# Output steps two places earlier, quadratic scores first, a drain in another order and logits in eight matmuls

## The reference

```
x = LN(x + linear_attention(x))           # 8 heads, elu+1 features, relu MLP
x = LN(x + moe64(x))                      # 64 experts, top 8 of 64, capacity 64 tokens each, shared expert
x = LN(x + gated_attention(x))            # below
x = LN(x + moe8(x))                       # 8 experts, top 2 of 8, all experts for all tokens
```

```
v, gate = split(silu(norm(x) @ Wh + bh))             # 256 features each
quad_q, lin_q, quad_k, lin_k = four affine copies of silu(norm(x) @ Wqk + bqk)
attn = relu(quad_q @ quad_k.T / 32 + bias)**2        # inside a group, lower triangle
out  = attn @ v + lin_q @ (sum over earlier groups of lin_k.T @ v / 32)
x    = (gate * out) @ Wout + bout + x
```

```
p = softmax(x @ Wg.T); top 2, normalised to sum 1 -> comb[t, e]
for e in 8 experts: a, b = split(x @ W1[e].T + b1[e]);  out += comb[:, e] * ((a * sigmoid(b)) @ Wo.T + bo)
```

## Time and profile before

| | us |
|---|---|
| median of 3 runs (lowest, highest) | 703.17 (703.03, 703.64) |
| the profiled execution | 702.37 |
| its span | 700.6 |
| PE busy | 587.2 (84%) |
| DVE busy | 437.3 (62%) |
| POOL busy | 442.0 (63%) |
| ACT busy | 274.0 (39%) |
| mean granted TensorE clock | 0.852 |

### The profile page before, as it was taken

One profiled execution on the slowest core, in us unless ns is written; L12 is line 12 of the kernel. 1 busy time (PEld: TensorE's weight loads), 2 busy tenths in 40 slices (PEclk: granted clock), 3 DMA queues, 4 the chain that ended last, 5 costly groups with the idle time before them and its releaser, 6 DMA issues.

```text
span 700.6 us, 10473 instructions
## 1 busy us (share of the span) xinstructions
PE 587.2 (84%) x3201; PEld 473.7 (68%) x3201; DVE 437.3 (62%) x1480; ACT 274.0 (39%) x559; POOL 442.0 (63%) x479
## 2 busy tenths in 40 slices
PE   5998999379299986365999989988989899999882
PEld 4797888335188775255777777867877787788662
DVE  2465778689634435534576767667667666775762
ACT  3465565215122223331634435345435353363331
POOL 6353444617677775644777867967868859652573
PEclk9999899659755555587999989999989989999996
DMA  4697475579022124330300300300203000000000
GB/s 121 175 300 292 190 270 220 195 170 206 10 72 65 60 67 146 124 120 1 121 1 9 127 1 8 128 9 13 115 8 127 1 8 8 1 16 0 10 7 16
DMA packets 47221, 61.98 MB, mean 88 GB/s; under 512 B 13026, under 2 KB 39873, under 8 KB 46146
## 3 DMA queue, kind: packets, MB, share of 16 engines
q1 hardware_dynamic: 44610, 56.15, 25.3%
q0 software_dynamic: 2560, 5.23, 2.6%
HBM read 35.16 MB, written 24.13 MB: 85 GB/s over the span
## 4 chain that ended last, share of the span: by engine, by line
PE 57%; DVE 18%; issue 8%; ACT 8%; DMA 4%; POOL 3%; SPq 1%; DVEq 0%; POOLq 0%; ACTq 0%
PE pair L1218 8%; PE pair L1220 7%; PE pair L1219 7%; PE pair L1450 5%; DVE c_g L1071 3%; DVE cand L1649 3%; PE pair L1460 2%; DVE keyT L1651 2%; PE pair L1324 2%; PE pair L467 2%; PE pair L1313 2%; PE pair L1717 2%; PE pair L1318 2%; ACT c_sg L940 2%; PE pair L511 2%
## 5 line engine op out<-in xcount | busy, mean ns | idle before, releaser
L854 POOL TENSOR_TENSOR c_acc<-c_acc,c_g 128x512 f32<-128x512 f32 x112 | 144.0, 1286 | 65.9 <-DVE c_g L1071 60.4
L940 ACT ACTIVATE c_sg<-pair 128x512 f32<-128x512 f32 x128 | 76.4, 597 | 161.6 <-PE pair L1220 161.3
L1071 DVE SCALAR_TENSOR_TENSOR c_g<-pair,c_comb,c_sg 128x256 f32<-128x256 f32 x224 | 97.6, 478 | 63.9 <-ACT c_sg L940 62.7
L1218 PE MATMUL pair<-c_w_hi,c_x3h 128*128 128x512 f32 x256 | 117.0, 457 | 9.3 <-DVE c_g L1071 6.6
L1220 PE MATMUL pair<-c_w_hi,c_x3l 128*128 128x512 f32 x256 | 105.8, 413 | 0.0
L1219 PE MATMUL pair<-c_w_lo,c_x3h 128*128 128x512 f32 x256 | 105.6, 412 | 0.0
L1218 PEld LDWEIGHTS pair<-c_w_hi,c_x3h 128*128 128x128 f32 x256 | 52.0, 203 | 25.6 <-DVE c_g L1071 13.4
L1220 PEld LDWEIGHTS pair<-c_w_hi,c_x3l 128*128 128x128 f32 x256 | 51.1, 200 | 12.7
L1219 PEld LDWEIGHTS pair<-c_w_lo,c_x3h 128*128 128x128 f32 x256 | 52.1, 204 | 8.0
L1534 POOL DMA_INDIRECT rows_all<-token_rows,tok_row x32 | 31.2, 976 | 12.6 <-issue 8.2
L1539 POOL DMA_INDIRECT routed_rows<-x1T_all,dest_row x32 | 32.3, 1008 | 9.8 <-issue 8.5
(11 more groups left out here) (326 smaller groups left out, 1499.0 us busy)
## 6 DMA issues: line engine op xcount, KB each, us to landing
routed_rows<-rows_all SPq DMA_DIRECT2D x8, 2048.0 KB
c_c<-routed_rows SPq DMA_DIRECT2D x7, 2048.0 KB, 7.7
token_rows<-a_xw SPq DMA_DIRECT2D x8, 384.0 KB, 3.1
a_x<-in_L_attn_x SPq DMA_DIRECT2D x8, 256.0 KB, 3.3
base_all<-a_xw SPq DMA_DIRECT2D x8, 256.0 KB, 3.5
c_c<-routed_rows SPq DMA_DIRECT2D x4, 512.0 KB, 5.1
out<-c_outb SPq DMA_DIRECT2D x16, 128.0 KB, 1.8
wgu_late<-in_L_ffn_w_gate SPq DMA_DIRECT2D x4, 480.0 KB, 7.1
```

The source lines that it names most:

```text
L854: g.tensor_tensor(acc, acc, b["g"][:, (2 * uf + i) % 4, :, :], ALU.add).then_inc(s["acc"], 1)
L940: a_.activation(b[f"sg{q % 2}"][:, :, :], self.pair[q % 2][:, :, H1:2 * H1], SIG).then_inc(s["sig"], 1)
L1071: ins = v.scalar_tensor_tensor(out=dst, in0=self.pair[q % 2][:, x, 0:H1], scalar=b[f"comb{uf}"][:, j * E1 + e:j * E1 + e + 1], in1=b[f"sg{ ...
L1218: t.matmul(dst, w_hi, x_hi, start=start, stop=False)
```

## The change

Seven things are done.

- **Output of half 0.** Its transposes go from place 10 to 8 and stand behind the value product there; its product with Wo and its half sums go from place 11 to 9, the product ahead of the w product. What belongs to half 1 stays.
- **Scores.** The four quadratic 128x128 matmuls come first, with a count of their own, and wait only for the products that they read; the linear ones follow. ACT does relu and square before it copies off1, which has its own semaphore now. `atd` goes from place 7 to 6.
- **Norm scale.** POOL computes the norm factors of half 1 of batch t behind the 128x1024 addition of the contributions instead of ahead of it.
- **Logits.** The high and low parts of Wg stand beside each other in one tile (`wg_hl`), so that the high part of x3 meets both in one matmul of 16 columns and the low part meets the high one in another of 8: eight matmuls, not twelve. DVE adds the two halves in a `tensor_reduce`, and the gating has 12 steps.
- **Drain.** For k >= 8, DVE does the aggregation ahead of the maxima and the norm additions ahead of the keys; in the last batch the shifted logits come behind the mask.
- **W1 on POOL.** `setup_pool_w1` waits for the last keys (`keys_written`).
- **Names.** Two blocks of PE's code become functions.

```diff
-AT = dict(zT=0, accT=(10, 1), out=(11, 2), gate=2, y4=(11, 3), quads=3, gate2=3, v=4, outb=(15, 5), sim=6, off=7, atd=7, av=8, w=9, x3=10, x3T=12, lg=13, y=7, z=11)
-
-GATING = {13: (1, 2, 3, 4), 14: (5, 6, 7, 8), 15: (9, 10, 11)}
-GATE_STEPS = 11
+AT = dict(zT=0, accT=(8, 1), out=(9, 2), gate=2, y4=(9, 3), quads=3, gate2=3, v=4, outb=(15, 5), sim=6, off=7, atd=6, av=8, w=9, x3=10, x3T=12, lg=13, y=7, z=11)
+
+GATING = {13: (1, 2, 3, 4, 5), 14: (6, 7, 8, 9), 15: (10, 11, 12)}
...
                     ins = v.match_replace(zap[:, j, :], b["top"][:, j, :], lg[:, j, :], NEG)
                 ins.then_inc(s["pick"], 1)
+
+            if k < self.N:
+                if 0 <= m < self.N:
+                    pick_top()
+                if 0 <= n < self.N:
+                    aggregate()
+            else:
+                if 0 <= n < self.N:
+                    aggregate()
+                if 0 <= m < self.N:
+                    pick_top()
+            if 0 <= m < self.N:
+                dve.wait_ge(s["pick"], 5 * m + 1)
+                if m < self.N - 1:
+                    from_top()
+                strike()
             n = k
             if n < self.N:
                 dve.wait_ge(s["kv_mm"], n + 1)
@@ -402,6 +423,8 @@
                 if m > 1:
                     dve.wait_ge(s["maskT_mm"], m // 2)
                 v.tensor_tensor(b["mask"][:, :, m % 2, :], zap, lg, ALU.not_equal).then_inc(s["mask_sb"], 1)
+                if m == self.N - 1:
+                    from_top()
             n = k - 1
             if 0 <= n < self.N:
                 dve.wait_ge(s["sqm_sb"], n + 1)
...
+
+            if k < self.N and 0 <= m and m % 2:
+                write_keys()
+            if 0 <= n < self.N:
+                add_norms()
+            if k >= self.N and m < self.N and m % 2:
+                write_keys()
 
     def pe(self, pe):
         t, b, s, bank, pair, ident = self.nc.tensor, self.b, self.s, self.bank, self.pair, self.ident
...
@@ -720,6 +752,7 @@
     def setup_pool_w1(self, pool):
         g, k, chain = self.nc.gpsimd, self.k, self.pool_chain
         pool.wait_ge(self.w1_loaded, 16)
+        pool.wait_ge(self.keys_written, PAIRS)
         chain(g.tensor_copy(k["w127"][:, :], k["w1n"][:, :, D - 1]))
         for q in range(4):
...
@@ -870,11 +903,12 @@
                 g.tensor_tensor(c[:, :, 0:512], c[:, :, 0:512], c[:, :, 512:1024], ALU.add).then_inc(s["sum_step"], 1)
             if f is not None:
                 add_experts(f, uf, 0, 1)
+            if not summed:
+                pool.wait_ge(s["sum_step"], 3 * r - 2)
+                g.tensor_tensor(c[:, :, 0:256], c[:, :, 0:256], c[:, :, 256:512], ALU.add).then_inc(s["sum_step"], 1)
             if t is not None:
                 rstd_f(t, 1)
             if not summed:
-                pool.wait_ge(s["sum_step"], 3 * r - 2)
-                g.tensor_tensor(c[:, :, 0:256], c[:, :, 0:256], c[:, :, 256:512], ALU.add).then_inc(s["sum_step"], 1)
                 pool.wait_ge(s["sum_step"], 3 * r - 1)
                 pool.wait_ge(s["z"], r)
                 yv = b["y"][:, :].rearrange("p (j d) -> p j d", d=D)
@@ -973,12 +1007,12 @@
                         act.wait_ge(s["gate_mm"], 3 * a + 3)
                         gate(a, 2, X)
                     if q == AT["sim"]:
-                        act.wait_ge(s["off_mm"], 2 * a + 1)
-                        a_.copy(b["off1"][:, :], Z[:, :])
                         act.wait_ge(s["t1"], a + 1)
                         a_.activation(b["rl"][:, :, :], b["t"][:, :, :], ACT.Relu).then_inc(s["relu"], 1)
                         act.wait_ge(s["relu"], a + 1)
                         a_.activation(b["rl"][:, :, :], b["rl"][:, :, :], ACT.Square).then_inc(s["t2"], 1)
+                        act.wait_ge(s["off_mm"], 2 * a + 1)
+                        a_.copy(b["off1"][:, :], Z[:, :]).then_inc(s["off1"], 1)
                     if q == AT["off"]:
                         act.wait_ge(s["off_mm"], 2 * a + 2)
...
@@ -1110,37 +1144,40 @@
             if step == 1:
                 dve.wait_ge(s["lg_mm"], a + 1)
                 v.memset(self.landing(), 0.0)
-                for j in range(NT):
-                    ins = v.max(top[:, j, :], t3(lg)[:, j, :])
+                ins = v.tensor_reduce(t3(lg), Z[:, 256:256 + 2 * n].rearrange("p (j h e) -> p j e h", h=2, e=E1), AX.X, ALU.add)
             else:
...
@@ -1174,12 +1211,12 @@
                         prod(a, 2, X, b["gateT"][:, 1, :])
                     if q == AT["sim"]:
 
-                        dve.wait_ge(s["diag_mm"], a + 1)
+                        dve.wait_ge(s["diag_mm"], 2 * a + 1)
                         t_, ml = b["t"][:, :, :], Y[:, :].rearrange("p (j i) -> p j i", i=P)
                         v.tensor_tensor(t_, X[:, :].rearrange("p (j i) -> p j i", i=P), bcast_mid(k["biasT"][:, :], NT), ALU.add).then_inc(s["t1"], 1)
+                        dve.wait_ge(s["diag_mm"], 2 * a + 2)
                         v.tensor_tensor(ml, ml, bcast_mid(k["ltmask"][:, :], NT), ALU.mult).then_inc(s["ml"], 1)
                     if q == AT["atd"]:
-                        t_, ml = b["t"][:, :, :], Y[:, :].rearrange("p (j i) -> p j i", i=P)
                         dve.wait_ge(s["ml"], a + 1)
                         dve.wait_ge(s["t2"], a + 1)
                         v.tensor_tensor(t_, b["rl"][:, :, :], ml, ALU.add).then_inc(s["atd"], 1)
@@ -1241,6 +1278,25 @@
                 tok = slice(j * P, (j + 1) * P)
                 ins = split3(self.pair[q % 2][:, x, :], b[f"x3h{uf}"][:, tok], b[f"x3l{uf}"][:, tok], b["w1_hi"][:, e, :], b["w1_lo"][:, e, :])
             ins.then_inc(s["u_mm"], 1)
+
+        def half_transposes(n, un, half):
+            pe.wait_ge(s["acc"], 14 * n + 7 * (half + 1))
+            if half or not first(n):
+                pe.wait_ge(s["outb"], 2 * n + half)
+            for x in range(2):
+                for h in range(2):
+                    c = slice((2 * x + h) * P, (2 * x + h + 1) * P)
+                    ins = t.transpose(bank[4][:, c], b[f"acc{un}"][:, 2 * half + x, h * P:(h + 1) * P], ident[:, :])
+            ins.then_inc(s["accT_mm"], 1)
+
...
@@ -1294,10 +1338,14 @@
                         split3(X[:, :], hi[:, HID + P:2 * HID], lo[:, HID + P:2 * HID], zh[:, :], zl[:, :]).then_inc(s["gate_mm"], 1)
                     if q == AT["sim"]:
                         pe.wait_ge(s["quads"], a + 1)
+                        pe.wait_ge(s["prod5"], 5 * a + 3)
+                        for j in range(NT):
+                            tok = slice(j * P, (j + 1) * P)
+                            ins = t.matmul(X[:, tok], b["qk"][:, tok], b["qq"][:, tok], start=True, stop=True)
+                        ins.then_inc(s["diag_mm"], 1)
                         pe.wait_ge(s["prod5"], 5 * a + 5)
                         for j in range(NT):
                             tok = slice(j * P, (j + 1) * P)
-                            t.matmul(X[:, tok], b["qk"][:, tok], b["qq"][:, tok], start=True, stop=True)
                             ins = t.matmul(Y[:, tok], b["lk"][:, tok], b["lq"][:, tok], start=True, stop=True)
                         ins.then_inc(s["diag_mm"], 1)
                         t.matmul(Z[:, 0:384], b["lk"][:, 0:P], b["lq"][:, P:L], start=True, stop=True)
@@ -1307,6 +1355,7 @@
                         t.matmul(X[:, 0:256], b["lk"][:, P:2 * P], b["lq"][:, 2 * P:L], start=True, stop=True).then_inc(s["off_mm"], 1)
                     if q == AT["av"]:
                         pe.wait_ge(s["atd"], a + 1)
+                        pe.wait_ge(s["off1"], a + 1)
                         pe.wait_ge(s["off2"], a + 1)
                         for h, dst in ((0, Y), (1, Z)):
                             c = slice(h * P, (h + 1) * P)
...
                                 ins = t.matmul(dst[:, j * P:(j + 1) * P], b["v"][:, j, c], b["t"][:, j, :], start=False, stop=(j == NT - 1), skip_group_check=True)
                             ins.then_inc(s["av_mm"], 1)
+                if f is not None and q == AT["accT"][0]:
+                    half_transposes(f, uf, 0)
+                if a is not None:
                     if q == AT["w"]:
                         pe.wait_ge(s["go"], 2 * a + 2)
                         for j in range(NT):
@@ -1333,7 +1385,9 @@
                         xh, xl = b[f"x3h{ua}"], b[f"x3l{ua}"]
                         for j in range(NT):
                             tok = slice(j * P, (j + 1) * P)
-                            ins = split3(Z[:, j * E1:(j + 1) * E1], xh[:, tok], xl[:, tok], k["wg_hi"][:, :], k["wg_lo"][:, :])
+                            at = 256 + j * 2 * E1
+                            t.matmul(Z[:, at:at + 2 * E1], xh[:, tok], k["wg_hl"][:, :], start=True, stop=False, skip_group_check=True)
+                            ins = t.matmul(Z[:, at:at + E1], xl[:, tok], k["wg_hl"][:, 0:E1], start=False, stop=True, skip_group_check=True)
                         ins.then_inc(s["lg_mm"], 1)
 
```

(12 more changed lines are left out.)

78 lines of the change are left out of this document (37 added, 41 removed).

## The result

The changed kernel takes 681.88 us, median of 4 runs (681.09 to 683.88), against 703.1 for the kernel before in the same comparison; the ratio is 0.9725, 95% interval 0.9686 to 0.9764. The profiled execution took 681.64, its span is 679.9, 20.7 less than the span before.

A forecast was written before the change was run, and what follows sets the result against it. Bodies bound by PE's matmuls, idle time and low clock; the first half by DVE's search and POOL's gathers. +2.5 - 4.5 - 0.85 - 4.9 - 8.8 + 2.7 = -13.85 from 702.37: 688.5, median 689; range 681 to 698.

The forecast's parts named there:

- Front, +2.5: Up to the first gather: last keys 2.05 us earlier, but POOL's W1 work waits for them, gather 2.5 us later.
- low pieces: Stretches of 3.41 us at granted clock 0.50; nine counted in the bodies, two taken to be left.
- Rival 2: POOL makes up its delay before the slots are ready, first gather 2 us earlier: 684.5 us; chance 0.09.
- First attention, -4.5: First attention body, uncovered by experts: split scores start the value product 3.6 us earlier, and part of its 1.7 is won.
- its logits, -0.85: First body's logits: four fewer matmuls at half clock save 0.85 us.
- Places 8 to 13, -4.9: Seven bodies at -0.7 us each: the 0.75 hole before the value product goes, smaller holes come at places 12 and 13.
- The walk: One body stepped through with its rows' durations: half sums ahead of y3 delay x3; logits at 557.2 instead of 557.90.
- Logits to transposes, -8.8: First logit to half-1 transposes, seven bodies: -12.0 us if the clock never falls, +3.2 for two low pieces left.
- Rivals 1, 3 and 4: Clock falls as before (692, chance 0.25); at place 12 and logits (about 700, 0.12); stays low between them (about 712, 0.04).
- Tail, +2.7: Ninth body: half-0 transposes at place 8 wait 2.5 us for POOL's seventh sum; bounds +2.1 and +3.5 (clock falls).

The follow-up runs named there:

- e7: The kernel before, run again with a trace and no edit: one run, 696.1 us.
- e5: The changed kernel without POOL's wait for the last keys: 677.14 us, ratio 0.9634.
- e3: The changed kernel with the scores in the old order (quadratic and linear alternating, off1 ahead of relu, atd at place 7): 693.9 us, ratio 0.9885.
- e2: The changed kernel with each 16-column logits matmul cut into two of 8 columns, twelve again: 681.92 us, ratio 0.9702.
- e1: The changed kernel with the output of half 0 back at places 10 and 11: 680.94 us, ratio 0.9701.
- e0: The changed kernel again, no edit: 682.86 us, ratio 0.9724.
- e9: e8 with the half sums of half 0 at place 11 instead of 9: 704.2 us, ratio 0.9826.
- e11: e8 with the half sums of half 0 at place 10 instead of 9: 710.87 us, ratio 0.9909.
- e4: The changed kernel with half 0's transposes and output back at places 10 and 11 in the ninth body only: 678.9 us, ratio 0.9665.
- e10: The kernel before with only the new order of the scores: 705.02 us, ratio 0.9819.
- e8: The changed kernel with the edits of e4 and e5 together: 692.6 us on a chip where before takes 719.15, ratio 0.9651.

## Why the prediction came out as it did

**Front, +2.5.** Right in mechanism and sign. The drain gained 1.65 (2.05 said), the new wait moved the gather from the slots to POOL, +1.63 at like clock (e7 against after), and the first normed transposes +2.1. The first trace of before had two low pieces at 70 us, worth 2.3 at the keys and 1.2 at the gather, which is why the two profiled executions differ by 0.4 there. Rival 2, POOL making up its delay, did not happen, and e5 puts the price of the wait at 3.

**First attention, -4.5, and its logits, -0.85.** Measured -4.3 and -0.86; e3 and e2 show that they are the scores and the four matmuls. In the other traces with the new scores first attention is 4.7 to 5.9 shorter, so that -4.3 is the least of them.

**Places 8 to 13, -4.9.** Measured -5.7, holes of 1.00, 0.37 and 0.71 where 1.25, 0.5 and 0.35 were said. The scores are 6.7 of it (e3), and the earlier output costs 1.0 the other way (e1 against e0). The walk had the half sums ahead of y3 as a cost. They are one, small, and what they free is larger: e9 and e11 show that either of the two next places makes a hole of 1.7 to 2.7.

**Logits to transposes, -8.8.** The term that was mis-sized: -12.6. Two bodies of before in e7 that ran at 1.00 throughout take 8.20 and 8.18 from logits to transposes, and the same bodies now 8.02 and 8.03: so about 1 us of the 12.6 is other than the clock, and nine low pieces cost the rest, 1.3 each, an estimate from these. The mechanism, no long hole and so no fall of the clock, holds in eight traces of eight with the half sums at place 9; I had left two of nine low pieces, and put the gain on the output as a whole, where e9 puts it on DVE's half sums; in six traces of six with a hole of 1.7 or more in each body there are four to nine. The two pieces left over stood on no row, and they are most of what the term missed. How the chip decides this the runs don't tell; single holes of 1.9 pass without a fall. The inner working was off too. I took off 0.45 for four matmuls and put on 0.45 for four transposes, and neither counts, as DVE paces this stretch (e2: under 0.1 a body on average); the errors cancel. Rivals 1, 3 and 4 had the clock fall in the seven bodies, and it did not. Rival 2's 684.5 is the nearest number to the time measured, but its mechanism did not happen.

**Tail, +2.7.** The wait was 2.30 (2.5 said), the whole 4.2 against the first trace, 3.9 against e4: the clock is low for 3.41 us right behind the wait, from 650.35 on, and the bound that I gave for that, +3.5, was 0.4 to 0.7 too low. The traces of e2 and e3 have the same wait of 2.3 and no low piece behind it, and take 32.17 us from the eighth body's transposes to the last ones, where after takes 33.51 and e4 29.62: so the wait costs 2.55, as said, and the clock 1.34.

**Not in the sum.** DVE's halt of 2.5 us at a loop turn, which was in the trace of before and which I did not ask about: -2.5. From the forecast's -13.85: logits to transposes -3.8, the halt -2.5, places 8 to 13 -0.8, the front -1.8, first attention +0.2, the second body's start +0.4, the tail +1.5 make -20.65, and the span shows -20.7.

**The noise.** The prediction had runs tell a change from none at 0.2%, from three runs within 0.6 us. The fourth was 697.78, and the interval of the comparison is 0.4% to either side.

## What to carry to other kernels

Look for the one long wait of TensorE in a repeated stage and for what its neighbour engine does just ahead of releasing it; work of that engine that nobody waits for soon belongs in front of the wait's chain, even where the walk shows new small holes. A move that is good where another stage covers it (output at place 8) can cost in the one iteration without cover; give that iteration its own place. And take a second trace of the kernel before ahead of a sum: of the 7 us that the forecast was off, 2.5 were a halt that comes in every trace of that kernel and 1.4 a low clock early on that came in one of two, and one trace can't tell which is which.

## What the hardware showed that I had not expected

The clock stayed at 1.00 for 321 us on end (329.5 to 650.3), with holes of up to 1.06 us in it; two traces of the same kernel differed by two low pieces in the first stage (6.8 us, 1.4 of them left at the first normed transposes). A DVE halt of 2.4 to 2.6 us, without a wait in the profile, comes at one turn of the loop over the bodies in both traces of before and in e10, and in no trace of the changed kernel or its variants. The experts' loop of the second layer was 17 us longer on the third chip, with ACT late in it (e8). The scatters there wait 19 us for DVE in e8, e9 and e10, where it is 1.2 in e4 and e5; the kernel before was 17 us slower on that chip too.
